# FP4 inner values turned by VectorE in 32x32 blocks and through HBM, their down-projection two chunks later, grid constants on ScalarE

## The chip, the cores and the metric

The kernel runs on one core of a Trainium2 chip. The metric is the device time of one execution in microseconds (us). Engines are named as in the profile: PE (TensorE) multiplies matrices, PEld is its weight load, DVE is VectorE, ACT is ScalarE, POOL is GpSimd, SP is the engine whose queue issues all DMAs here.

## The reference

Four batches of 1024 tokens with 256 features are layer-normed (xn). One branch is a linear attention with 8 heads and a gated network of 1024 inner values. The other is a gated network whose inputs, weights and inner values are rounded to FP4 in groups of 16. The output joins the two.

```python
def fp4_quant_dequant(x):                      # groups of 16 along the last dim
    scale = max(max(abs(group)) / 6.0, 1e-12)
    idx = searchsorted(_MID, abs(group / scale))
    return _GRID[idx] * sign(group) * scale    # grid 0, 0.5, 1, 1.5, 2, 3, 4, 6

xn = layernorm(x)
s  = x1 + silu(h @ Wgate) * (h @ Wup) @ Wdown  # x1 = xn + attention(rmsnorm(xn)), h = rmsnorm(x1), 1024 inner values
gate, y = fp4_linear(xn, w_gate), fp4_linear(xn, w_up)   # 704 inner values
g  = silu(fp4_linear(silu(gate) * y, w_down))  # the inner values are rounded to FP4 too
return x + s * g
```

## The kernel before

All matmuls work on values split in a high and a low part (HI, LO), three products for one: `split_product`, whose matmuls are line L248 in every view. The high part is rounded by ACT, the low part is what DVE subtracts.

The kernel has two stages. The first, some 610 us, goes through attention head by head; it also rounds the FP4 weights and the inputs and keeps what the second needs in HBM. The second, `networks`, goes through 8 blocks of 512 tokens (n), each of 4 chunks of 128 tokens (c). Of the plain network it makes two tiles of 128 inner values per chunk (f = 2c and 2c + 1, an even and an odd one, for all 512 tokens of the block); of the FP4 network it makes the 704 inner values of one chunk of tokens. Chunks of the FP4 network are numbered m = 4n + c, 0 to 31.

Each engine runs its own instruction list in the order written out by hand in `networks`; semaphores join them. One chunk on each engine:

- PE: `gate_up4` (FP4 gate and up, in two halves of 352 columns: two banks, B_GATE4 and B_UP4, each written by a half only when the half before was read, semaphores `s_gate4_ready` and `h4_ready`), `gate_up` of the even tile, `down` of the odd tile before, `turn4` (six 128x128 transposes of the quantized inner values of the chunk before, L759), `gate_up` of the odd tile, `down` of the even tile, `down4` (17 matmuls, FP4 down-projection of the chunk before).
- DVE: `product4` for both halves (L1440), `quantize_scale` (five steps, L1398 to L1402), `mlp_product` and `mlp_lo` of the even tile (L1429, L1433), `hq_lo` (L1446, low part of the turned chunk before, two parts), `quantize_constants` (L1406 takes the exponent bits, L1408 makes max(power, 1) * 1.5 * 2^22 of them, into `grid4`), `mlp_product` of the odd tile, `quantize_add` (L1411), `mlp_lo`, `quantize_subtract` (L1416), `quantize_done` (L1421 multiplies by the scale, L1422 repeats the last 64 columns). In chunk 0 the two halves of product4 for chunk 1 stand inside the chunk, ahead of `quantize_subtract` and at the end. Chunk 3 also has `xT_lo_of` (L1377, four operations on the next block's inputs) and the sum of the block with its residual (L1517).
- ACT: `silu4` (L1029), then for each tile silu of the gate and the rounding of the product (`mlp`, L1033 and L1035), `hq` (L1040, rounds the turned chunk), `gate_out` (L1046, silu of the FP4 network's output).
- POOL: products and sums of the output, four of each per block (L538, L542); at the start of the stage it makes the low part of `wdown` (L529).
- SP: loads the next inputs (`load_turned`, `load_xb`) and stores results.

At the end of the last block `last_down4` waits for the last chunk's transposes, and DVE makes the last products and sums. The steps that exchange blocks through HBM in the first stage (`exchange`: one store of 512 KB to `moved`, four loads of 128 KB) are of the kind that the change adds to the second.

Of the kernel before, what the change touches and what calls it, by code (L numbers as in the profile page):

```python
# [5 lines left out]
ALU = mybir.AluOpType  # L6
# [52 lines left out]
def build(nc, x, attn_w, Wq, Wk, Wv, Wo, out_w, mlp_w, Wgate, Wup, Wdown, w_gate, w_up, w_down, out):  # L59
# [32 lines left out]
                        for name in ("kept_xq", "kept_h2"))  # L92
    quant4 = nc.dram_tensor("quant4", (3 * NET4,), F32).ap()
# [5 lines left out]
    with ctx:  # L99
# [39 lines left out]
        eps = sb("eps", [P, 1], F32)  # L139
        warm = sb("warm", [P, 1], F32)  # L140
# [20 lines left out]
        x2 = one.cut(CH, ROW)  # L161
        state = one.cut(CH - 1, P)
# [35 lines left out]

        def as_tokens(row):
            return row.rearrange("p (c b t) -> p c b t", c=CH, b=QUADS)  # L200
# [28 lines left out]
        x2b = two.cut(CH, ROW)  # L229
        two.at = 0  # L230
# [96 lines left out]
        h4_turned, hq_hi, hqT_ready = sem("h4_turned"), sem("hq_hi"), sem("hqT_ready")  # L327
        out4_done, g4_ready = sem("out4_done"), sem("g4_ready")
# [4 lines left out]
        FIRST4 = min(T4, CH)  # L333
        FULL4, REST4 = N4 // P, N4 % P
# [17 lines left out]
        with nc.Block() as block:  # L352
            @block.sync
            def _(sp):
# [114 lines left out]
                def load_xb(n):  # L469
# [14 lines left out]
                sp.wait_ge(wdown_ready, 1)  # L484
                load_xb(0)
                sp.wait_ge(h2_turned, BLOCKS + 1)
                sp.dma_start(kept_h2[BLOCKS - 1].rearrange("a p x -> p a x"), leaving.rearrange("p a i x -> p a (i x)"))\
                  .then_inc(h2_stored, 16)

                for n in range(BLOCKS - 1):  # L490
                    if n + 2 < BLOCKS:
                        sp.wait_ge(xT_ready, (n + 1) * TURNS + KD)
                        load_turned(xq_in, kept_xq[n + 2], xq_loaded)
                        sp.wait_ge(xT_ready, (n + 1) * TURNS + TURNS)
                        sp.wait_ge(h2_stored, 16 * (n + 4))
                        load_turned(h2_in, kept_h2[n + 2], h2_loaded)
                    sp.wait_ge(res_ready, n + 1)
                    sp.dma_start(out_blocks[n], res).then_inc(out_stored, 16)
                    load_xb(n + 1)
# [7 lines left out]
            def _(pool):  # L507
                pool.memset(ident[:, :], 0.0).then_inc(s_const, 1)
                pool.memset(causal[:, :, :], 1.0).then_inc(s_const, 1)
                pool.memset(eps[:, :], EPS).then_inc(s_const, 1)  # L510
                pool.memset(leaving[:, :, 1, :], 0.0).then_inc(leaving_clear, 1)
                pool.wait_ge(s_const, 3)
# [15 lines left out]
                pool.wait_ge(wdown_hi, 1)  # L528
                pool.tensor_tensor(wdown[:, LO, :, :], raw_wdown, wdown[:, HI, :, :].bitcast(F32),  # L529
                                   ALU.subtract).then_inc(wdown_ready, 1)  # L530
# [15 lines left out]
            def _(pe):  # L546
# [44 lines left out]
                pe.wait_ge(s_const, 5)  # L591
# [131 lines left out]
                def down(n, f):  # L723
                    if f == 0:
                        pe.wait_ge(sum_read, n + 1)
                        pe.wait_ge(wdown_ready, 1)
                    pe.wait_ge(hmT_ready, n * FT + f + 1)
# [25 lines left out]
                def turn4(n, c):  # L753
                    pe.wait_ge(h4_quantized, n * CH + c + 1)
                    for f in range(T4):
                        if f == FIRST4:
                            pe.wait_ge(g4_ready, n * CH + c + 1)
                        bank = B_TURN4 if f < FIRST4 else B_OUT4
                        done = pe.transpose(ps[:, bank, (f % CH) * P:(f % CH + 1) * P],  # L759
                                            h4[:, c % 2, f * P:(f + 1) * P], ident[:, :])  # L760
# [3 lines left out]
                def down4(n, c):  # L764
                    pe.wait_ge(hqT_ready, (n * CH + c) * 2 + 2)
# [9 lines left out]
                def last_down4(n, c):  # L775
                    for f in range(T4):
                        if f in (0, FIRST4):
                            pe.wait_ge(hq_hi, (n * CH + c) * 2 + (1 if f == 0 else 2))
# [4 lines left out]
                    for f in range(T4):  # L783
                        if f in (0, FIRST4):
                            pe.wait_ge(hqT_ready, (n * CH + c) * 2 + (1 if f == 0 else 2))
# [36 lines left out]
                def networks(n, final):  # L822

                    for c in range(CH):
# [3 lines left out]
                        if c:  # L828
                            down(n, 2 * c - 1)
                            turn4(n, c - 1)  # L830
                        gate_up(n, 2 * c + 1)
                        down(n, 2 * c)
                        if c:
                            down4(n, c - 1)
                    down(n, FT - 1)
                    turn4(n, CH - 1)
                    if not final:
                        gate_up4(n + 1, 0)
                        down4(n, CH - 1)
                    else:  # L840
                        last_down4(n, CH - 1)
# [5 lines left out]
            def _(act):  # L847
# [104 lines left out]
                act.wait_ge(s_const, 5)  # L952
# [78 lines left out]
                def mlp(n, f):  # L1031
                    act.wait_ge(gate_done, n * FT + f + 1)
                    act.activation(s_gate, ps[:, B_GATE, :], ACT.Silu).then_inc(s_gate_ready, 1)  # L1033
                    act.wait_ge(hm_ready, n * FT + f + 1)
                    act.activation(hmT[:, f % 2, HI, :], hm, ACT.Copy).then_inc(hm_hi, 1)  # L1035

                def hq(n, c):
                    for i, (bank, f0, f1) in enumerate(((B_TURN4, 0, FIRST4), (B_OUT4, FIRST4, T4))):
                        act.wait_ge(h4_turned, (n * CH + c) * 2 + i + 1)
# [4 lines left out]
                def gate_out(n, c, bank=B_OUT4):  # L1044
                    act.wait_ge(out4_done, n * CH + c + 1)
                    act.activation(g4[:, c, :], ps[:, bank, 0:D], ACT.Silu).then_inc(g4_ready, 1)  # L1046
# [19 lines left out]
                act.activation(wdown[:, HI, :, :], raw_wdown, ACT.Copy).then_inc(wdown_hi, 1)  # L1066
                normed_h2(BLOCKS + 1, xq_new)

                def networks(n, final):
                    for c in range(CH):  # L1070
                        if c:
                            silu4(n, c)
                        mlp(n, 2 * c)
                        if c:
                            hq(n, c - 1)
                        if c == CH - 1 and not final:
                            xT_hi_of(n + 1, range(KD))
                        mlp(n, 2 * c + 1)
                        if c:
                            if c == 1:  # L1080
                                act.wait_ge(product_ready, n * CH + 1)
                            gate_out(n, c - 1)
# [478 lines left out]
```

## Time and profile before

| what | value |
|---|---|
| median of 3 runs | 1111.18 us (1109.03 to 1113.21) |
| profiled execution, its own time | 1108.42 us |
| its span | 1106.7 us |
| PE busy in the span | 1083.8 us (98%) |
| DVE busy | 906.8 us (82%) |
| ACT busy | 511.8 us (46%) |
| POOL busy | 52.2 us (5%) |
| granted clock of PE | 1.0 |

The views give times in us from the span's start. A row of the view in order of time has the start, the duration, the engine, the line, what is written from what, how many instructions were merged, and in brackets how long the engine stood idle before and who ended that. Matmuls are pipelined, so the distance between the starts of two groups tells what a group takes.

### The profile page before, as it was taken

To read this page: it belongs to the slowest core of one execution; us is meant where nothing else is said; L and a number is where in the kernel's file an instruction comes from. 1 tells how busy PE (TensorE), PEld (TensorE's weight loads), DVE (VectorE), ACT (ScalarE), POOL (GpSimd) and SP (SyncE) were. 2 spreads that over 40 slices of the span, in tenths; PEclk is the share of its full clock that TensorE was granted. 3 is DMA by queue.
4 is the path that set the end of the run, shared out by engine and by line. 5 is a ranking of instruction groups with operands and counts; after the bars stand their busy time and mean duration, and the time that the engine had idled before them with its cause. 6 is when DMAs were issued, how large, how long until landed. Compare 5 with 4: busy or idle time off the path is not lost.

```text
span 1106.7 us, 18820 instructions
## 1 busy us (share of the span) xinstructions
PE 1083.8 (98%) x7016; PEld 985.9 (89%) x7016; DVE 906.8 (82%) x1978; ACT 511.8 (46%) x1422; POOL 52.2 (5%) x71
## 2 busy tenths in 40 slices
PE   9999999999999999999998799999999999999997
PEld 6998999999989989999987699999999999999897
DVE  6888888898888988998677878878878778787786
ACT  6654646546546465465554533233323333233332
POOL 0000000000000000000000102020010202020200
PEclk9999999999999999999999999999999999999999
DMA  7455355454553554535447402011110203030010
GB/s 236 147 167 166 112 186 162 143 183 130 179 163 126 168 162 158 183 116 166 145 146 205 110 20 71 25 39 58 39 58 20 77 2 96 1 95 1 17 42 20
DMA packets 113466, 120.01 MB, mean 108 GB/s; under 512 B 8672, under 2 KB 108384, under 8 KB 113376
## 3 DMA queue, kind: packets, MB, share of 16 engines
q1 hardware_dynamic: 113376, 118.82, 34.0%
q8 instruction: 55, 0.90, 0.4%
q14 instruction: 35, 0.29, 0.1%
HBM read 65.75 MB, written 53.04 MB: 107 GB/s over the span
## 4 chain that ended last, share of the span: by engine, by line
PE 79%; DVE 12%; DMA 5%; ACT 2%; issue 1%; SPq 1%; POOL 0%; DVEq 0%; POOLq 0%
PE ps L248 59%; PE ps L638 4%; PE ps L679 4%; PE ps L673 4%; PE ps L659 3%; DMA moved<-work 3%; DMA r_gate<-moved 2%; PE ps L759 2%; PE ps L590 1%; DVE work L1429 1%; DVE r_k L1377 1%; DVE r_v L1433 1%; SPq L385 1%; DVE r_v L1446 1%; DVE work L1402 1%
## 5 line engine op out<-in xcount | busy, mean ns | idle before, releaser
L248 PE MATMUL ps<-r_k,r_gate_up 128*128 128x512 f32 x768 | 187.6, 394 | 4.0 <-DVE work L1429 3.3
L248 PEld LDWEIGHTS ps<-r_k,r_gate_up 128*128 128x128 f32 x768 | 141.0, 188 | 32.1 <-DVE work L1429 3.7
L248 PE MATMUL ps<-r_o,onT 128*128 128x256 f32 x768 | 107.0, 288 | 0.1
L898 ACT ACTIVATE work<-ps 128x128 f32<-128x128 f32 x256 | 67.4, 278 | 81.4 <-PE ps L679 81.4
L248 PEld LDWEIGHTS ps<-r_q,r_v 128*128 128x128 f32 x768 | 99.5, 191 | 5.9 <-issue 2.1
L248 PE MATMUL ps<-hT,r_k 128*128 128x512 f32 x378 | 103.2, 408 | 0.0
L248 PE MATMUL ps<-r_q,r_v 128*128 128x256 f32 x768 | 102.7, 283 | 0.0
L1035 ACT ACTIVATE r_v<-work 128x512 fp32r<-128x512 f32 x64 | 40.5, 633 | 131.9 <-DVE work L1429 131.9
L248 PE MATMUL ps<-hT,r_q 128*128 128x512 f32 x384 | 98.2, 391 | 0.0
L248 PE MATMUL ps<-r_v,hT 128*128 128x512 f32 x384 | 97.4, 390 | 0.0
L248 PEld LDWEIGHTS ps<-r_o,onT 128*128 128x128 f32 x768 | 95.7, 190 | 0.3 <-DVE onT L1157 0.3
L874 ACT ACTIVATE work<-ps 128x512 f32<-128x512 f32 x64 | 38.3, 599 | 121.8 <-PE ps L248 121.6
L248 PEld LDWEIGHTS ps<-hT,r_q 128*128 128x128 f32 x384 | 72.1, 188 | 16.4
L248 PEld LDWEIGHTS ps<-r_v,hT 128*128 128x128 f32 x384 | 72.1, 188 | 15.0
L1440 DVE TENSOR_TENSOR work<-ps,work 128x352 f32<-128x352 f32 x64 | 33.5, 523 | 56.9 <-PE ps L248 54.4
L248 PEld LDWEIGHTS ps<-hT,r_k 128*128 128x128 f32 x378 | 66.4, 189 | 11.1
L248 PE MATMUL ps<-r_gate,r_k 128*128 128x352 f32 x384 | 72.4, 324 | 2.7 <-ACT work L1029 2.7
L248 PE MATMUL ps<-r_up,r_k 128*128 128x352 f32 x384 | 72.3, 324 | 0.0
L679 PE MATMUL ps<-work 128*128 128x128 f32 x448 | 65.6, 284 | 3.9 <-DVE work L1347 2.9
L673 PE MATMUL ps<-work 128*128 128x128 f32 x512 | 67.7, 275 | 0.2 <-DVE work L1323 0.2
L638 PE MATMUL ps<-work 128*128 128x128 f32 x512 | 67.4, 274 | 0.0
L1033 ACT ACTIVATE work<-ps 128x512 f32<-128x512 f32 x64 | 38.3, 599 | 60.6 <-PE ps L248 60.6
(147 smaller groups left out, 2047.4 us busy)
## 6 DMA issues: line engine op xcount, KB each, us to landing
moved<-work SPq DMA_DIRECT2D x63, 512.0 KB, 2.9
r_gate<-moved SPq DMA_DIRECT2D x252, 128.0 KB, 2.6
work<-in_L_attn_hidden_states SPq DMA_DIRECT2D x16, 512.0 KB, 5.4
kept<-work SPq DMA_DIRECT2D x9, 514.0 KB, 4.4
kept_h<-work SPq DMA_DIRECT2D x9, 512.0 KB, 3.7
work<-kept SPq DMA_DIRECT2D x8, 514.0 KB, 6.1
kept_xq<-work SPq DMA_DIRECT2D x8, 512.0 KB, 5.8
work<-kept_xq SPq DMA_DIRECT2D x32, 128.0 KB, 2.8
```

The lines of the kernel that those rows point to most:

```text
L248: done = pe.matmul(out_ap, a, b, start=first and n == 0, stop=last and n == 2, skip_group_check=skip)
L385: sp.dma_start(arriving[q * QUAD:(q + 1) * QUAD].rearrange("p a i x -> p a (i x)"), moved[q].rearrange("(a p) x -> p a x", a=QUADS)).then_ ...
L638: done = pe.matmul(ps[:, B_SCORE, c * P:(c + 1) * P], kT[:, c * P:(c + 1) * P], qT[:, j % 2, c * P:(c + 1) * P], start=True, stop=True)
L659: done = pe.matmul(ps[:, B_STATE, c * P:(c + 1) * P], k_tok[:, c, :], v_sb[:, half, c, hv:hv + P], start=True, stop=True)
L673: pe.matmul(ps[:, B_O, c * P:(c + 1) * P], attn[:, c, :], v_sb[:, half, c, hv:hv + P], start=c == 0, stop=s == 0 and c == 0, skip_group_ch ...
L679: done = pe.matmul(ps[:, B_O, c * P:(c + 1) * P], qT[:, j % 2, c * P:(c + 1) * P], before, start=False, stop=True, skip_group_check=True)
L759: done = pe.transpose(ps[:, bank, (f % CH) * P:(f % CH + 1) * P], h4[:, c % 2, f * P:(f + 1) * P], ident[:, :])
L874: act.activation(kT, ps[:, B_K, :], ACT.Copy).then_inc(k_ready, 1)
L898: done = act.activation(squares[:, c, :], ps[:, B_O, c * P:(c + 1) * P], ACT.Square, accum_out=small[:, OS, c:c + 1])
L1033: act.activation(s_gate, ps[:, B_GATE, :], ACT.Silu).then_inc(s_gate_ready, 1)
L1035: act.activation(hmT[:, f % 2, HI, :], hm, ACT.Copy).then_inc(hm_hi, 1)
L1440: dve.tensor_tensor(h4[:, c % 2, e * HALF4:(e + 1) * HALF4], ps[:, B_UP4, 0:HALF4], s_gate4[:, e, :], ALU.mult).then_inc(h4_ready, 1)
```

## The change

- `turn4` goes. In `quantize_done` DVE turns the rescaled chunk itself, in blocks of 32x32 with two transposes (640 columns, and the last 64 columns read twice for 128); SP stores the result to a buffer in HBM (`kept_h4`, two of them in turn) and loads it back in four parts with the blocks in their turned places (`exchange4`). The last chunk, m = 31, is still turned by PE (`last_turn4`).
- `down4` of a chunk runs two chunks later (LAG4 = 2), so `hq`, `hq_lo` and `gate_out` do too. `hq` and `hq_lo` are one operation of 768 columns each, from SBUF. `gate_out` of a block's first chunk waits for the output products of the block before.
- `grid4` is made by ACT (`grid4_on_act`: Relu(power * GRID - GRID), the bias from a column of memory), behind the even tile's work and ahead of the odd tile's silu. DVE adds GRID back in the add and the subtract, which become two-step operations; the sign is turned by the subtract, and the scale is made negative for it.
- The low part of `wdown` is made by DVE in two halves instead of POOL, and ACT rounds it in two halves.
- SP's order is written anew around `exchange4`.

```diff
+                def exchange4(m):
+                    through = kept_h4[m % 2]
+                    sp.wait_ge(h4_quantized, m + 1)
+                    sp.dma_start(through.rearrange("a p x -> p a x"), h4_turned_sb).then_inc(hq_stored, 16)
+                    sp.wait_ge(hq_stored, 16 * (m + 1))
+                    if m:
+                        sp.wait_ge(hqT_ready, m)
+                    for q in range(QUADS):
+                        sp.dma_start(hq_in[q * QUAD:(q + 1) * QUAD],
+                                     through[q].rearrange("(b p) x -> p b x", b=QUADS)).then_inc(hq_loaded, 16)
+                for n in range(BLOCKS):
+                    exchange4(n * CH)
...
+                    exchange4(n * CH + 1)
+                    if n:
+                        sp.wait_ge(res_ready, n)
+                        sp.dma_start(out_blocks[n - 1], res).then_inc(out_stored, 16)
+                        load_xb(n)
+                    exchange4(n * CH + 2)
...
-                pool.tensor_tensor(wdown[:, LO, :, :], raw_wdown, wdown[:, HI, :, :].bitcast(F32),
-                                   ALU.subtract).then_inc(wdown_ready, 1)
...
-                            turn4(n, c - 1)
                         gate_up(n, 2 * c + 1)
                         down(n, 2 * c)
-                        if c:
-                            down4(n, c - 1)
+                        if n * CH + c >= LAG4:
+                            down4(n * CH + c - LAG4)
                     down(n, FT - 1)
-                    turn4(n, CH - 1)
                     if not final:
                         gate_up4(n + 1, 0)
-                        down4(n, CH - 1)
                     else:
-                        last_down4(n, CH - 1)
+                        for m in range(LAST4 + 1 - LAG4, LAST4):
+                            down4(m)
+                        last_turn4()
+                        last_down4()
...
+                def hq(m):
+                    act.wait_ge(hq_loaded, 16 * QUADS * (m + 1))
+                    if m:
+                        act.wait_ge(out4_done, m)
+                    act.activation(hqT[:, HI, :, :].rearrange("p f (a t) -> p f a t", t=QUAD), turned4_sb(hq_in), ACT.Copy)\
+                       .then_inc(hq_hi, 1)
+                def grid4_on_act(m):
+                    act.wait_ge(power4_ready, m + 1)
+                    act.activation(grid4, grid4, ACT.Relu, scale=GRID, bias=minus_grid[:, 0:1]).then_inc(grid4_ready, 1)
...
-                    settled2(dve.tensor_scalar(grid4.bitcast(U32), data.bitcast(U32), EXPONENT, None,
-                                               ALU.bitwise_and), mine)
-                    settled2(dve.tensor_scalar(grid4, grid4, 1.0, 1.5 * 2.0 ** 22, ALU.max, ALU.mult), mine)
+                    dve.tensor_scalar(grid4.bitcast(U32), data.bitcast(U32), EXPONENT, None,
+                                      ALU.bitwise_and).then_inc(power4_ready, 1)
...
-                    dve.tensor_tensor(data, data, grid4, ALU.add).then_inc(dve2, 1)
+                    dve.wait_ge(grid4_ready, m + 1)
+                    dve.scalar_tensor_tensor(data, grid4, GRID, data, ALU.add, ALU.add).then_inc(dve2, 1)
...
+                    dve.transpose(to[:, 0:FULL4], data[:, 0:split].rearrange("p (f a t) -> p f a t", a=QUADS, t=QUAD))
+                    rest = data[:, split:N4].rearrange("p (d a t) -> p d a t", d=1, t=QUAD)
+                    dve.transpose(to[:, FULL4].rearrange("p (d a) t -> p d a t", d=2),
+                                  rest.to_broadcast([P, 2, QUADS // 2, QUAD])).then_inc(h4_quantized, 1)
...
+                def wdown_lo(i):
+                    dve.wait_ge(wdown_hi, i + 1)
```

DVE's list for a chunk 1, from the even tile's mlp_product to the end of the chunk. Before:

```order
L1429 TENSOR_TENSOR work<-ps,work 128x512
L1433 TENSOR_TENSOR r_v<-work,r_v 128x512
L1446 TENSOR_TENSOR r_v<-ps,r_v 128x512
L1446 TENSOR_TENSOR r_v<-ps,r_v 128x256
L1406 TENSOR_SCALAR work<-work 128x704
L1408 TENSOR_SCALAR work<-work 128x704
L1429 TENSOR_TENSOR work<-ps,work 128x512
L1411 TENSOR_TENSOR work<-work 128x704
L1433 TENSOR_TENSOR r_v<-work,r_v 128x512
L1416 TENSOR_TENSOR work<-work 128x704
L1421 TENSOR_TENSOR work<-work 128x704
L1422 COPY work<-work 128x64
```

DVE's list at the same place, now (L1500 is mlp_product, L1504 mlp_lo, L1516 hq_lo, L1467 the mask):

```order
L1500 TENSOR_TENSOR work<-ps,work 128x512
L1504 TENSOR_TENSOR r_v<-work,r_v 128x512
L1516 TENSOR_TENSOR r_v<-work,r_v 128x768
L1467 TENSOR_SCALAR work<-work 128x704
L1500 TENSOR_TENSOR work<-ps,work 128x512
L1472 SCALAR_TENSOR_TENSOR work<-work 128x704
L1504 TENSOR_TENSOR r_v<-work,r_v 128x512
L1477 SCALAR_TENSOR_TENSOR work<-work 128x704
L1482 TENSOR_TENSOR work<-work 128x704
L1490 STREAM_TRANSPOSE work<-work 128x5x4x32
L1492 STREAM_TRANSPOSE work<-work 128x4x32
```

The multiply L1408 left the list, the two parts of hq_lo became one, and two transposes stand at the end in the place of the copy.

ACT's list for a chunk without extras, from silu4 to gate_out. Before:

```order
L1029 ACTIVATE work<-ps 128x352 x2
L1033 ACTIVATE work<-ps 128x512
L1035 ACTIVATE r_v<-work 128x512
L1040 ACTIVATE r_v<-ps 128x512
L1040 ACTIVATE r_v<-ps 128x256
L1033 ACTIVATE work<-ps 128x512
L1035 ACTIVATE r_v<-work 128x512
L1046 ACTIVATE work<-ps 128x256
```

ACT's list at the same place, now (L1069 is the silu of a tile, L1079 hq, L1084 the grid):

```order
L1065 ACTIVATE work<-ps 128x352 x2
L1069 ACTIVATE work<-ps 128x512
L1079 ACTIVATE r_v<-work 128x768
L1073 ACTIVATE r_v<-work 128x512
L1084 ACTIVATE work<-work,minus_grid 128x704
L1069 ACTIVATE work<-ps 128x512
L1073 ACTIVATE r_v<-work 128x512
L1098 ACTIVATE work<-ps 128x256
```

The grid stands between the even tile's rounding and the odd tile's silu, and hq moved ahead of the even tile's rounding.

PE's list at the end of the program, from the last chunk's second gate_up. Before:

```order
L248 MATMUL ps<-r_k,r_gate_up 128x512 x12
L248 MATMUL ps<-r_q,r_v 128x256 x12
L248 MATMUL ps<-r_o,r_v 128x256 x15
L771 MATMUL ps<-r_o,r_v 128x256 x2
L248 MATMUL ps<-r_q,r_v 128x256 x12
L759 MATMUL ps<-ident,work 128x128 x6
L781 MATMUL ps<-r_o,r_v 128x256 x11
L786 MATMUL ps<-r_o,r_v 128x256 x6
```

PE's list at the same place, now:

```order
L258 MATMUL ps<-r_k,r_gate_up 128x512 x12
L258 MATMUL ps<-r_q,r_v 128x256 x12
L258 MATMUL ps<-r_o,r_v 128x256 x15
L807 MATMUL ps<-r_o,r_v 128x256 x2
L258 MATMUL ps<-r_q,r_v 128x256 x12
L258 MATMUL ps<-r_o,r_v 128x256 x15
L807 MATMUL ps<-r_o,r_v 128x256 x2
L794 MATMUL ps<-ident,work 128x128 x6
L817 MATMUL ps<-r_o,r_v 128x256 x11
L822 MATMUL ps<-r_o,r_v 128x256 x6
```

A down4, that of chunk 30, came between the last mlp product and the last chunk's transposes.

## Rows read from the trace of the kernel before

**Rows 1.** Busy time of each engine in a stretch of the second stage, all engines:

```profile
core 0: us, PE busy (x) PEld busy (x) DVE busy (x) ACT busy (x) POOL busy (x), PEclk, DMA share, GB/s
645.00:1090.00 445.00, 443.62 (x2808) 409.99 (x2807) 346.96 (x598) 149.14 (x294) 43.92 (x56) 1.00 0.13 40
```

**Rows 2.** In order of time, PE, one chunk: start, us, operation, idle:

```profile
828.89 2.91 PE L248 MATMUL ps<-r_k,r_gate_up 128*128 128x512 f32 x12
831.64 1.60 PE L248 MATMUL ps<-r_q,r_v 128*128 128x256 f32 x12
833.07 0.81 PE L759 MATMUL ps<-ident,work 128*128 128x128 f32 x6
833.64 3.01 PE L248 MATMUL ps<-r_k,r_gate_up 128*128 128x512 f32 x12
836.49 1.60 PE L248 MATMUL ps<-r_q,r_v 128*128 128x256 f32 x12
```

**Rows 3.** In order of time, DVE, the same chunk:

```profile
827.19 0.53 DVE L1440 TENSOR_TENSOR work<-ps,work 128x352 f32<-128x352 f32 x1 [1.10 <-PE ps L248]
829.09 0.53 DVE L1440 TENSOR_TENSOR work<-ps,work 128x352 f32<-128x352 f32 x1 [1.38 <-PE ps L248]
829.65 0.89 DVE L1398 TENSOR_REDUCE work<-work 128x44 f32<-128x704 f32 x1
...
832.40 0.69 DVE L1429 TENSOR_TENSOR work<-ps,work 128x512 f32<-128x512 f32 x1
833.79 0.69 DVE L1433 TENSOR_TENSOR r_v<-work,r_v 128x512 fp32r<-128x512 f32 x1 [0.70 <-ACT r_v L1035]
834.40 1.01 DVE L1446 TENSOR_TENSOR r_v<-ps,r_v 128x512 fp32r<-128x512 f32 x2
835.33 0.52 DVE L1406 TENSOR_SCALAR work<-work 128x704 uint32<-128x704 uint32 x1
...
836.75 0.69 DVE L1429 TENSOR_TENSOR work<-ps,work 128x512 f32<-128x512 f32 x1 [0.34 <-PE ps L248]
...
839.68 0.89 DVE L1421 TENSOR_TENSOR work<-work 128x704 f32<-128x704 f32 x1
...
842.09 0.53 DVE L1440 TENSOR_TENSOR work<-ps,work 128x352 f32<-128x352 f32 x1 [1.28 <-PE ps L248]
```

**Rows 4.** In order of time, DVE, sums of two blocks, inputs of the next:

```profile
676.88 1.22 DVE L1517 TENSOR_TENSOR work<-ps,work 128x1024 f32<-128x1024 f32 x1
...
850.23 1.29 DVE L1377 TENSOR_TENSOR r_k<-work,r_k 128x512 fp32r<-128x512 f32 x2
...
857.72 1.22 DVE L1517 TENSOR_TENSOR work<-ps,work 128x1024 f32<-128x1024 f32 x1
```

**Rows 5.** Groups by line and shape, whole span: count, busy us, mean ns, idle:

```profile
L1224 DVE STREAM_TRANSPOSE work<-work 128x512 f32<-128x512 f32 x34 | 21.5, 672 | 0.0
L1188 DVE SCALAR_TENSOR_TENSOR r_gate_up<-work,nw_mlp,r_gate_up 128x512 fp32r<-128x512 f32 x8 | 5.9, 741 | 0.0
L922 ACT ACTIVATE work<-work 128x256 f32<-128x256 f32 x36 | 15.2, 496 | 0.0
L943 ACT ACTIVATE r_o<-work,nw_out 128x2048 fp32r<-128x2048 f32 x1 | 2.0, 2007 | 0.0
```

**Rows 6.** In order of time, POOL and DVE, where they meet:

```profile
744.89 2.80 POOL L542 TENSOR_TENSOR work<-work 128x256 f32<-128x256 f32 x4
...
747.28 0.97 DVE L1433 TENSOR_TENSOR r_v<-work,r_v 128x512 fp32r<-128x512 f32 x1 [0.70 <-ACT r_v L1035]
```

**Rows 7.** DMA issues by line: count, KB each, median us from issue to landing:

```profile
moved<-work SPq DMA_DIRECT2D x63, 512.0 KB, 2.9
r_gate<-moved SPq DMA_DIRECT2D x252, 128.0 KB, 2.6
```

**Rows 8.** In order of time, POOL and DVE, the start of the second stage:

```profile
619.37 4.56 POOL L529 TENSOR_TENSOR r_q<-work,r_q 128x2048 fp32r<-128x2048 f32 x1 [26.04 <-ACT r_q L1066]
...
620.13 3.85 DVE L1399 TENSOR_SCALAR work<-work 128x44 f32<-128x44 f32 x1
```

More of the change, by code:

```diff
@@ L161, in build @@
         x2 = one.cut(CH, ROW)
+        x2_end = one.at
         state = one.cut(CH - 1, P)
@@ L197, in landed, with turned4_sb @@
             return tile.rearrange("p (b k c t) -> p k c b t", b=QUADS, k=KD, c=CH)[:, k]
+        def turned4_sb(tile):
+            return tile.rearrange("p a (f t) -> p f a t", t=QUAD)
         def as_tokens(row):
@@ L229, in build @@
         x2b = two.cut(CH, ROW)
+        two.at = max(two.at, x2_end)
+        h4_turned_sb = two.cut(QUADS, T4 * QUAD)
+        hq_in = work[:, down4_at:down4_at + QUADS * T4 * QUAD].rearrange("p (a x) -> p a x", a=QUADS)
         two.at = 0
@@ L333, in build @@
         FIRST4 = min(T4, CH)
+        LAG4 = 2
+        LAST4 = BLOCKS * CH - 1
         FULL4, REST4 = N4 // P, N4 % P
@@ L726, in down @@
                         pe.wait_ge(wdown_ready, 1)
+                    if n == 0 and f == FT // 2:
+                        pe.wait_ge(wdown_ready, 2)
                     pe.wait_ge(hmT_ready, n * FT + f + 1)
@@ L1042, in hq, with gate_out @@
                            .then_inc(hq_hi, 1)
-                def gate_out(n, c, bank=B_OUT4):
-                    act.wait_ge(out4_done, n * CH + c + 1)
-                    act.activation(g4[:, c, :], ps[:, bank, 0:D], ACT.Silu).then_inc(g4_ready, 1)
+                def gate_out(m, bank=B_OUT4):
+                    if m % CH == 0 and m:
+                        act.wait_ge(product_ready, m + 1)
+                    act.wait_ge(out4_done, m + 1)
+                    act.activation(g4[:, m % CH, :], ps[:, bank, 0:D], ACT.Silu).then_inc(g4_ready, 1)
                 def weights4_hi(i, k):
@@ L1065, in _ @@
                 act.wait_ge(wdown_loaded, 16)
-                act.activation(wdown[:, HI, :, :], raw_wdown, ACT.Copy).then_inc(wdown_hi, 1)
+                for f in range(0, FT, FT // 2):
+                    act.activation(wdown[:, HI, f:f + FT // 2, :], raw_wdown[:, f:f + FT // 2, :], ACT.Copy)\
+                       .then_inc(wdown_hi, 1)
                 normed_h2(BLOCKS + 1, xq_new)
@@ L1070, in networks @@
                     for c in range(CH):
+                        earlier = n * CH + c - LAG4
                         if c:
                             silu4(n, c)
-                        mlp(n, 2 * c)
-                        if c:
-                            hq(n, c - 1)
+                        silu_gate(n, 2 * c)
+                        if LAG4 == 2 and earlier >= 0:
+                            hq(earlier)
+                        hmT_hi(n, 2 * c)
                         if c == CH - 1 and not final:
                             xT_hi_of(n + 1, range(KD))
[L1078 to L1082, printed above, removed]
+                        grid4_on_act(n * CH + c)
+                        silu_gate(n, 2 * c + 1)
+                        if LAG4 == 1 and earlier >= 0:
+                            hq(earlier)
+                        hmT_hi(n, 2 * c + 1)
+                        if earlier >= 0:
+                            gate_out(earlier)
                     if not final:
                         xT_hi_of(n + 1, range(KD, TURNS))
-                    hq(n, CH - 1)
-                    if not final:
                         silu4(n + 1, 0)
-                    gate_out(n, CH - 1, B_GATE if final else B_OUT4)
+                    else:
+                        for m in range(LAST4 + 1 - LAG4, LAST4):
+                            hq(m)
+                            gate_out(m)
+                        last_hq()
+                        gate_out(LAST4, B_GATE)
                 for n in range(BLOCKS - 1):
@@ L1477, in _ @@
                 product4(0, 0, 1)
+                def wdown_lo(i):
+                    dve.wait_ge(wdown_hi, i + 1)
+                    part = slice(i * FT // 2, (i + 1) * FT // 2)
+                    dve.tensor_tensor(wdown[:, LO, part, :], raw_wdown[:, part, :], wdown[:, HI, part, :].bitcast(F32),
+                                      ALU.subtract).then_inc(wdown_ready, 1)
+                wdown_lo(0)
                 DVE_BLOCK = CH * (SCALE_STEPS + ROUND_STEPS)
@@ L1512, in networks @@
                     if final:
-                        hq_lo(n, CH - 1)
+                        for m in range(LAST4 + 1 - LAG4, LAST4):
+                            hq_lo(m)
+                        last_hq_lo()
                     dve.wait_ge(mlp_done, n + 1)
@@ L1519, in networks @@
                     if not final:
-                        hq_lo(n, CH - 1)
                         product4(n + 1, 0, 0)
```

104 lines of the change are left out of this document (63 added, 41 removed).

## The prediction, made before the changed kernel was run

> **What bounds the kernel now.** I read the busy times of the second stage first (the networks, some 445 of 1106.7 us): PE is busy for 443.6 of 445 us, DVE for 347, ACT for 149 [rows 1]. So PE sets the pace there, and a matmul taken off PE is time won, as long as nobody else becomes the pace. DVE's 78% looks like room. Whether it is room is not told by a share but by the order, so next I read one chunk in order of time on PE and on DVE.
>
> PE: twelve 512-column products take 2.75 us (828.89 to 831.64), twelve 256-column products 1.43, the six transposes 0.57 (833.07 to 833.64), and the twelve 512-column products behind them 2.85, 0.10 more than the others [rows 2]. A transposed chunk thus costs PE 0.67 us. DVE: from one chunk's first product4 to the next is 14.90 us (827.19 to 842.09), and in it DVE waits 1.28 and 1.38 us for PE at product4's halves, 0.34 at the second mlp_product, and 0.70 for ACT at mlp_lo [rows 3]. A block of four chunks takes (857.72 - 676.88) / 3 = 60.28 us [rows 4]. So DVE's real room is about 3 us in a chunk, and only where it waits for PE.
>
> **The change, part by part.** All times are for the steady blocks; there are seven periods from block to block.
>
> *PE loses turn4*: 0.67 us per chunk. PE alone would need 14.90 - 0.67 = 14.23 per chunk, 56.9 per block.
>
> *DVE, one chunk walked again in the new order*, from product4's first half to the next chunk's first half. The first half (0.53) frees the bank, PE makes the second up product (half of the 1.90 between 827.19 and 829.09, 0.95), and DVE starts 0.20 after its end (829.09 against 828.89): 1.68 when DVE comes last, where 1.90 was PE's pace. Second half 0.56, scales 2.75, mlp_product and ACT's rounding 1.39, mlp_lo 0.61, all as before [rows 2, 3]. hq_lo is one operation of 768 columns: from 512 columns at 0.69 and 704 at 0.89 [rows 3] a column is 1.04 ns, so 0.96, less 0.08 that operations in a row overlap (0.69 long, 0.61 apart): 0.88, where the two parts took 0.93. The mask takes 0.52 as before.
>
> Then comes **the new wait**. ACT makes the grid constants only when the mask is there, and silu_gate of the odd tile is queued behind it on ACT, so mlp_product of that tile waits on DVE for both. The grid is 704 columns with a pointer: 256 such columns take 0.496, 2048 take 2.007, so 0.84 ns a column and 0.87 us [rows 5]. silu_gate is another ACT operation of 512 columns, 0.70 with both hops, as the wait at 833.79 shows [rows 3]; operations in a row overlap a little, so I take 1.50 together. Before, mlp_product waited 0.34 for PE there and ACT had its silu ready. The multiply taken from DVE (from the mask's end at 835.85 to 836.41, where that wait begins: 0.56) gives back a third of this. Queued behind the wait on DVE are the whole rounding, the transposes and the next chunk's product4, for which PE's up product waits.
>
> Product, add, mlp_lo, subtract: 2.93 (836.75 to 839.68), with the add and the subtract in their two-step form taken as equal; the nearest row is 0.741 against 0.69 at 512 columns, so up to 0.06 more for each [rows 3, 5]. Rescaling 0.92. The transposes: 512 columns take 0.672 [rows 5], so 640 take 0.81 and 128 take 0.27, less the overlap 0.91 together; before, the copy of 64 columns hid in the wait for PE. Sum: 1.68 + 0.56 + 2.75 + 1.39 + 0.61 + 0.88 + 0.52 + 1.50 + 2.93 + 0.92 + 0.91 = **14.65**. That is over PE's 14.23: DVE's round now sets the pace, and PE waits for h4_ready.
>
> *The block.* Chunks 0 and 1 have one product4 round trip between them, since chunk 1's halves are made inside chunk 0: 2 x 14.65 - (1.68 + 0.56) + 0.44 + 0.55 = 28.05. Within chunk 0 PE's own way to that product is 0.53 + 0.95 + 5.50 + 1.43 + 2.03 (17 matmuls at 0.12) + 1.90 + 0.20 = 12.54 after product4, and DVE is there at 11.90, so 0.64 more: 28.69. Chunk 2: 14.65. Chunk 3 has four xT_lo of 0.60 and the sum of 1.13 besides [rows 4]: 18.2. Together 61.5.
>
> *POOL.* Its products and sums of the output now come one chunk later, and the last product meets DVE in back-to-back operations on two SBUF operands. Today four sums run from 744.89 to 747.69, and mlp_lo that starts at 747.28 takes 0.97 instead of 0.69: it stood still until POOL was done [rows 3, 6]. That is 0.28 today, in time DVE had to spare. I take one POOL instruction of 0.7 (2.80 / 4) in DVE's way per block, so 0.6; bounds 0 and 2.
>
> By the Trainium skill (SBUF — State Buffer, "SBUF: two separate sides") whoever starts first holds the shared ports for a whole instruction, and it names two-operand VectorE operations against GpSimd's; the row above agrees. By it the worst case is all five instructions, 5 x 0.7 = 3.5 per block; whether a transpose is held up too no row here shows.
>
> So a block takes 61.5 + 0.6 = 62.1, against 60.28: +1.85, and +13 over seven.
>
> *The exchange* through HBM is hidden. A store takes 2.9 us and loads 2.6 [rows 7]; the loads wait for hq_lo of the chunk before, and ACT needs them one chunk later less hq_lo's own way there (rounding, mlp_lo, hq_lo, some 4 us), so about 10 us cover 2.6 and the issue of four. If that cover went, each us beyond it would cost 1 us in each of 31 chunks. SP's other transfers (res, x, the turned inputs) stand between the exchanges, with a chunk or more to their use.
>
> *Start*: today POOL's 4.56 us for wdown's low part holds a DVE scalar operation of 44 columns for 3.85 [rows 8]. The change gives that back, but puts two halves of 1024 columns (1.2 each, at 1.04 ns a column) on DVE, and chunks 0 and 1 of block 0 have the new wait and the transposes too. I take 0, within 2 either way. *Tail*: down4 of chunk 30 now stands between the last mlp product and the last chunk's transposes, with its hq_lo ahead of it: 2.03 + 0.88 = 2.9.
>
> Sum: 13 + 0 + 2.9 = **+16 us**. The profiled execution (1108.42, span 1106.7) would be 1124; it ran 2.8 under the median of 1111.18, so the median comes to **1127**.
>
> By the Trainium skill (VectorE: DVE Perf Modes, "Rules for kernel authors") a 128x128 transpose belongs on TensorE when PSUM may take it, which speaks against the change. Op for op the trace agrees: 0.67 on PE against 0.91 on DVE; it doesn't decide, since PE is the full engine today.
>
> **Rivals.**
> *DVE's room is enough, PE stays the bound.* For it: 3 us of waits per chunk on DVE today. The block is then 56.9, 3.4 less, times seven plus the tail: 1111 - 24 + 3 = 1090. It needs a DVE round of at most 14.23 in every chunk and room for the block's extras (3.5 us), so some 1.2 us less per chunk than I count; it would hold if silu of the odd tile didn't stand behind the grid on ACT. It does in ACT's order. Chance 0.07.
> *A tie.* Transposes at 0.72 (the small one hidden), the grid at 0.79, no POOL in the way: 0.27 less per chunk and 0.6 per block, a block of 60.4, and the tail remains: 1115. Chance 0.14.
> *Worse.* The transposes write pieces of 32 columns far apart; should they take 1.3, two-step add and subtract 0.06 more each and POOL 2 per block, the block is 62.1 + 4 x 0.5 + 1.4 = 65.5: 1111 + 37 + 3 = 1151; half of that 1139. Chance 0.11.
>
> **How the numbers follow.** My forecast, DVE's round with the wait for ACT as the bound, has 0.68 and 1127, with its own ends at about 1117 and 1137. The range 1113 to 1139 leaves out the first rival, the low half of the tie and the far half of the worse case, about 0.2. Within 0.5% (5.6 us, about what a measurement of this kernel can tell from none) lie most of the tie and little else: same 0.13; faster is the first rival, 0.07; slower 0.80.
>
> **What would show it.** In the trace of the changed kernel: mlp_product of the odd tile waits about 1.5 us for ACT's silu in each chunk, where it waited 0.34 for PE; product4's first half of chunks 2 and 3 no longer waits for PE, and PE waits there for product4; the block's sum on DVE comes every 62 us; PE is busy for less than 97% of the stage. hq on ACT waits for no transfer. I'm wrong if product4 still waits over 0.5 us for PE in its first half (then PE is the bound and the time falls), if ACT waits for the loads, or if the transposes take much other than 0.8 and 0.27.

## The result, and the profile after

The changed kernel takes 1137.49 us (median, 1136.23 to 1140.1) where the kernel before takes 1110.11 in the same comparison: 1.0261 times as long, interval 1.024 to 1.0281. It is slower, as forecast, by 27 us where 16 were forecast. Its profiled execution took 1136.23 us, with a span of 1134.5 us.

The busy times of the second stage, the view of [rows 1], here for the changed kernel (the columns are the same; the last two stretches are 2 and 3.5 us of one chunk):

```profile
core 0: us, PE busy (x) PEld busy (x) DVE busy (x) ACT busy (x) POOL busy (x), PEclk, DMA share, GB/s
650.00:1100.00 450.00, 417.41 (x2494) 376.03 (x2492) 340.02 (x540) 160.06 (x280) 52.00 (x56) 0.98 0.28 85
...
834.90:836.90 2.00, 1.98 (x7) 1.98 (x8) 0.00 (x0) 0.00 (x0) 0.44 (x1) 0.50 0.55 197
836.80:840.30 3.50, 3.50 (x14) 2.84 (x14) 3.04 (x6) 1.26 (x2) 0.00 (x0) 0.81 0.02 5
```

PE is busy for 92.8% of the stage, where it was 99.7%: it is no longer what sets the pace. DVE is at 76% and doesn't look full either. As in [rows 1], the share hides what the order shows. DVE in order of time, from the even tile's mlp_product of chunk 1 to the scales of the next chunk, answers [rows 3]:

```profile
823.72 0.69 DVE L1500 TENSOR_TENSOR work<-ps,work 128x512 f32<-128x512 f32 x1
825.11 0.69 DVE L1504 TENSOR_TENSOR r_v<-work,r_v 128x512 fp32r<-128x512 f32 x1 [0.70 <-ACT r_v L1073]
825.72 0.95 DVE L1516 TENSOR_TENSOR r_v<-work,r_v 128x768 fp32r<-128x768 f32 x1
826.59 0.52 DVE L1467 TENSOR_SCALAR work<-work 128x704 uint32<-128x704 uint32 x1
828.61 0.69 DVE L1500 TENSOR_TENSOR work<-ps,work 128x512 f32<-128x512 f32 x1 [1.50 <-ACT work L1069]
829.22 0.88 DVE L1472 SCALAR_TENSOR_TENSOR work<-work 128x704 f32<-128x704 f32 x1
830.02 0.68 DVE L1504 TENSOR_TENSOR r_v<-work,r_v 128x512 fp32r<-128x512 f32 x1
830.62 1.43 DVE L1477 SCALAR_TENSOR_TENSOR work<-work 128x704 f32<-128x704 f32 x1
832.08 1.30 DVE L1482 TENSOR_TENSOR work<-work 128x704 f32<-128x704 f32 x1
833.42 0.84 DVE L1490 STREAM_TRANSPOSE work<-work 128x640 f32<-128x640 f32 x1
834.19 0.27 DVE L1492 STREAM_TRANSPOSE work<-work 128x128 f32<-128x128 f32 x1
834.38 0.48 DVE L1511 TENSOR_TENSOR work<-ps,work 128x352 f32<-128x352 f32 x1
837.09 0.53 DVE L1511 TENSOR_TENSOR work<-ps,work 128x352 f32<-128x352 f32 x1 [2.22 <-PE ps L258]
```

Three things are to be seen. The odd tile's mlp_product waits 1.50 us for silu (ACT L1069), where it waited 0.34 for PE. The first half of product4 (834.38) waits for nobody, where it waited 1.10 and 1.28 for PE. And the subtract and the rescaling take 1.43 and 1.30 us here, where the same two-step form takes 0.88 in the add two rows above and the rescaling took 0.89 before. Beside them POOL is at work, seen in order of time:

```profile
830.32 0.98 POOL L571 TENSOR_TENSOR work<-work 128x256 f32<-128x256 f32 x1 [13.43 <-ACT work L1098]
831.26 4.07 POOL L575 TENSOR_TENSOR work<-work 128x256 f32<-128x256 f32 x4
```

The subtract starts beside the last product, the rescaling runs beside the sums. The same four sums took 2.80 in [rows 6]. PE in order of time, the place that waits for product4's first half, with the same place of the block before ahead of it (the rows of [rows 2] no longer have their twin, since the transposes are gone):

```profile
771.59 1.23 PE L258 MATMUL ps<-r_up,r_k 128*128 128x352 f32 x6 [2.45 <-DVE work L1511]
772.65 2.91 PE L258 MATMUL ps<-r_k,r_gate_up 128*128 128x512 f32 x12
775.40 1.60 PE L258 MATMUL ps<-r_q,r_v 128*128 128x256 f32 x12
...
831.36 1.11 PE L258 MATMUL ps<-r_gate,r_k 128*128 128x352 f32 x6
834.92 2.13 PE L258 MATMUL ps<-r_up,r_k 128*128 128x352 f32 x6 [2.45 <-DVE work L1511]
836.85 3.51 PE L258 MATMUL ps<-r_k,r_gate_up 128*128 128x512 f32 x12
840.20 1.60 PE L258 MATMUL ps<-r_q,r_v 128*128 128x256 f32 x12
```

Both times PE stands idle for 2.45 us. At 771.59 it goes on as it was: the six matmuls take 1.06 (to 772.65), the twelve behind them 2.75. At 834.92 the six take 1.93 and the twelve 3.35, at a granted clock of 0.50 in the first 2 us (the second stretch of the table above): the lower of the two levels, 1.2 GHz instead of 2.4. DVE's second half, which needs the six, then waits 2.22, where it waited 1.32 after 771.59.

Where the slow stretch lies differs from block to block. In the block ahead of these two, PE goes on at 707.14 after the same wait; the six matmuls still take 1.06, and the twelve behind them 4.34. DVE then waits for the twelve, at the even tile's mlp_product:

```profile
712.80 0.69 DVE L1500 TENSOR_TENSOR work<-ps,work 128x512 f32<-128x512 f32 x1 [1.13 <-PE ps L258]
```

The block sum (L1606) starts at 675.26, 739.70, 803.05, 867.36, 931.87, 996.32, 1060.78 and 1127.43. So a block takes (1060.78 - 675.26) / 6 = 64.25 us, against 60.28 [rows 4]; 63.35 in the one block without the clock's fall, 64.3 to 64.5 in the five others. The last block, which is not among the six, has a fall too (granted clock 0.50 from 1095 to 1097).

### The profile page after: what moved, and what is told of

It reads as the page before. It is cut to its first block, busy times and chain, and to the rows that moved or that the text cites. A ratio compares the mean times of both kernels' runs of the same rounds, so it can differ in the third digit from the quotient of the medians.

```text
span 1134.5 us, 18698 instructions
## 1 busy us (share of the span) xinstructions
PE 1079.8 (95%) x6830; PEld 974.0 (86%) x6830; DVE 914.4 (81%) x1948; ACT 533.6 (47%) x1424; POOL 55.7 (5%) x71
## 4 chain that ended last, share of the span: by engine, by line
PE 65%; DVE 25%; ACT 5%; issue 3%; DMA 2%; SPq 0%; DVEq 0%
PE ps L258 47%; PE ps L671 5%; PE ps L706 4%; PE ps L712 4%; PE ps L692 4%; DVE work L1482 2%; DVE work L1500 2%; DVE work L1477 2%; DVE r_v L1504 2%; DVE work L1511 2%; DVE r_k L1438 2%; DVE work L1463 1%; DVE work L1459 1%; ACT work L1084 1%; DVE r_v L1516 1%
## 5 line engine op out<-in xcount | busy, mean ns | idle before, releaser
L258 PE MATMUL ps<-r_k,r_gate_up 128*128 128x512 f32 x768 | 198.3, 409 | 2.1 <-DVE work L1500 2.0
L258 PEld LDWEIGHTS ps<-r_k,r_gate_up 128*128 128x128 f32 x768 | 148.6, 199 | 36.4 <-DVE work L1500 7.6
L258 PE MATMUL ps<-r_up,r_k 128*128 128x352 f32 x384 | 76.7, 337 | 26.6 <-DVE work L1511 26.6
L258 PEld LDWEIGHTS ps<-r_up,r_k 128*128 128x128 f32 x384 | 63.8, 193 | 31.9 <-DVE work L1511 31.2
L1500 DVE TENSOR_TENSOR work<-ps,work 128x512 f32<-128x512 f32 x64 | 44.2, 691 | 54.6 <-ACT work L1069 48.2
L1069 ACT ACTIVATE work<-ps 128x512 f32<-128x512 f32 x64 | 37.7, 589 | 98.8 <-PE ps L258 98.8
L706 PE MATMUL ps<-work 128*128 128x128 f32 x512 | 67.7, 275 | 0.2 <-DVE work L1384 0.2
L712 PE MATMUL ps<-work 128*128 128x128 f32 x448 | 65.1, 283 | 2.8 <-DVE work L1408 2.7
```

Of the source, the lines that this page charges most:

```text
L258: done = pe.matmul(out_ap, a, b, start=first and n == 0, stop=last and n == 2, skip_group_check=skip)
L706: pe.matmul(ps[:, B_O, c * P:(c + 1) * P], attn[:, c, :], v_sb[:, half, c, hv:hv + P], start=c == 0, stop=s == 0 and c == 0, skip_group_ch ...
L712: done = pe.matmul(ps[:, B_O, c * P:(c + 1) * P], qT[:, j % 2, c * P:(c + 1) * P], before, start=False, stop=True, skip_group_check=True)
L1500: dve.tensor_tensor(hm, ps[:, B_UP, :], s_gate, ALU.mult).then_inc(hm_ready, 1)
```

## The experiments

Two theories are held against each other. **A**: DVE's round is the pace, made too long above all by the wait for silu behind the grid; POOL and PE's clock add to it. **B**: the new operations themselves are what costs (the turning on DVE, the exchange, the two-step forms), wherever silu stands. Kernels that undo or mend one part are told as edits of the changed kernel, those that make one part alone as edits of the kernel before. The kernel before took 1107.83 us beside four of them (silu ahead of the grid, grid back on DVE, no POOL, filler on PE) and 1109.35 beside the other four.

**silu ahead of the grid on ACT.** (The added wait is one that is always met by then.)

```diff
-                        grid4_on_act(n * CH + c)
                         silu_gate(n, 2 * c + 1)
+                        grid4_on_act(n * CH + c)
...
+                    if f % 2:
+                        dve.wait_ge(hmT_ready, n * FT + f)
```

> The changed kernel with one line moved on ScalarE: the odd tile's silu ahead of the grid constants. Theory A (VectorE's round is the pace, and the grid in front of the odd tile's silu is its largest new part): the 1.5 us wait of mlp_product in each chunk falls to about 0.3 at the add, a chunk's round from 14.65 to about 13.4, under TensorE's 14.23; a block comes down from 64.4 to 58.5 to 60, the time to 1093 to 1108, no slower than the kernel before. Rival B (the turning itself is the loss, by VectorE's transposes, the transfers and what they hold up): a block stays over 62.5, the time over 1122.

It took 1104.01 us, ratio 0.9965 (0.9942 to 0.9989); a block takes 59.93 (671.41 to 791.26, two blocks). DVE, the same place as above, odd tile's mlp_product to product4:

```profile
815.29 0.68 DVE L1502 TENSOR_TENSOR work<-ps,work 128x512 f32<-128x512 f32 x1
816.33 0.89 DVE L1472 SCALAR_TENSOR_TENSOR work<-work 128x704 f32<-128x704 f32 x1 [0.36 <-ACT work L1084]
817.14 0.68 DVE L1506 TENSOR_TENSOR r_v<-work,r_v 128x512 fp32r<-128x512 f32 x1
817.74 0.88 DVE L1477 SCALAR_TENSOR_TENSOR work<-work 128x704 f32<-128x704 f32 x1
818.66 1.31 DVE L1482 TENSOR_TENSOR work<-work 128x704 f32<-128x704 f32 x1
```

mlp_product waits no more, and the grid now comes 0.36 late for the add. That is 1.14 less in each of four chunks, PE's wait in chunk 2 is 0.77 instead of 2.45, no fall of the clock follows it, and a block is 4.3 us shorter than the changed kernel's 64.25. B is out as the main cause: turning, exchange and two-step forms are all still there. DVE is still late in places: the 0.77 us are a wait for product4 (up product at 821.51).

**The grid back on DVE**, the rest of the change as it is:

```diff
-                        grid4_on_act(n * CH + c)
...
+                    settled2(dve.tensor_scalar(grid4, grid4, 1.0, GRID, ALU.max, ALU.mult), mine)
...
-                    dve.scalar_tensor_tensor(data, grid4, GRID, data, ALU.add, ALU.add).then_inc(dve2, 1)
+                    dve.scalar_tensor_tensor(data, grid4, 0.0, data, ALU.add, ALU.add).then_inc(dve2, 1)
```

> The changed kernel with the grid constants made by VectorE again (two operations, as before), all else as changed: blocks turned through HBM, down-projection two chunks later. A: the wait of 1.5 goes, 0.56 of work comes back, a chunk's round 13.7; a block about 60, the time 1102 to 1110, about the kernel before. B: the turning alone is slower than before by 15 us or more.

1108.15 us, ratio 0.9993 (0.9968 to 1.0018), block 60.41 (672.41 to 793.24, two). So turning on DVE with the exchange neither costs nor wins, within 0.3% and with the wdown part in it, which is worth some 2 us by itself (below). The groups of PE by shape, from 676 us on, say why nothing is won:

```profile
L258 PE MATMUL ps<-r_up,r_k 128*128 128x352 f32 x324 | 61.8, 326 | 12.9 <-DVE work L1510 12.9
```

PE has no transposes left, but it waits 12.9 us for product4, some 2.0 in a block (0.97 in chunk 0 and 1.00 in chunk 2): most of the 4 x 0.67 that it was given goes into waiting.

**The grid on ACT alone**, in the kernel before: `grid4_on_act(n * CH + c)` ahead of `mlp(n, 2 * c + 1)`, and the add and the subtract in their two-step forms.

> The kernel before with the grid constants on ScalarE alone (as in the change, ahead of the odd tile's silu; two-step add and subtract), transposes on TensorE, down-projection one chunk later as before. A: the wait adds some 0.9 to VectorE's chunk, which the 1.1 to 1.3 of its wait for TensorE at product4 takes in; only at the block's end, where TensorE waits for the quantized chunk 3, it shows: 0 to 0.9 per block, the time 1107 to 1115. If the wait costs its length wherever it stands: 31 x 0.9 = 28 more, 1136.

1116.02 us, ratio 1.0073 (1.0045 to 1.0101), block 61.43 (675.39 to 798.26, two), 1.15 more than before: a little past the 0.9 and the 1115 us that I expected at most. The wait is the same one, as DVE in order of time shows; the first row is the first half of a product4, the second the odd tile's mlp_product after it:

```profile
828.74 0.53 DVE L1449 TENSOR_TENSOR work<-ps,work 128x352 f32<-128x352 f32 x1 [0.38 <-PE ps L249]
...
838.90 0.69 DVE L1438 TENSOR_TENSOR work<-ps,work 128x512 f32<-128x512 f32 x1 [1.50 <-ACT work L1037]
```

Here product4 still waits for PE (0.38 where it was 1.10): the wait for silu was paid for the most part out of DVE's room. Taken apart, then, the turning (with the rest of the change) costs nothing and the grid on ACT 0.7%; together they cost 2.6%. Each alone about fits into the same room of DVE, and both don't.

**wdown's low part on DVE alone**, in the kernel before:

```diff
-                pool.tensor_tensor(wdown[:, LO, :, :], raw_wdown, wdown[:, HI, :, :].bitcast(F32),
-                                   ALU.subtract).then_inc(wdown_ready, 1)
...
+                wdown_lo(0)
```

> The kernel before with only the low part of wdown made by VectorE in two halves instead of GpSimd. The prediction took the start at 0, within 2. A: the 3.85 us stand of the 44-column operation goes, 2.3 of work come: the time 1 to 3 less, 1105 to 1107. If two halves on VectorE cost more than the stand: 1108 to 1111.

1106.98 us, ratio 0.9979 (0.9964 to 0.9994). The first block, from the second half of its first product4 to its sum, takes 56.55 (617.43 to 673.98) where it took 58.23 before (618.65 to 676.88): this part of the change is worth some 2 us by itself.

**No POOL in blocks 0 to 6.** The kernel leaves out POOL's products and sums there, so the output of these blocks is not made; all waits and transfers stay.

```diff
-                        pool.tensor_tensor(res[:, c, :], res[:, c, :], g4[:, c, :], ALU.mult).then_inc(product_ready, 1)
+                        pool.sem_inc(product_ready, 1)
...
-                        done = pool.tensor_tensor(res[:, c, :], res[:, c, :], xb[:, c, :], ALU.add)
-                    done.then_inc(res_ready, 1)
+                    pool.sem_inc(res_ready, 1)
```

> The changed kernel without GpSimd's output products and sums in the blocks 0 to 6 (that part of the output is left out; all waits and transfers stay). A: the subtract and the rescaling of chunk 1 take 0.9 each instead of 1.43 and 1.30, TensorE's wait ahead of chunk 2's second up product falls from 2.45 to about 1.5, its clock stays at 2.4 GHz there, and a block takes 62.2 to 62.6 instead of 64.4: the time about 1123. If the clock falls all the same: about 63.4 and 1130. If GpSimd has no part in it: 1137.

1124.41 us, ratio 1.013 (1.0066 to 1.0194), block 62.41 (676.69 to 801.51, two). DVE's two operations are back at 0.89, PE waits 1.50 instead of 2.45, and no fall of the clock follows (DVE, then PE, in order of time):

```profile
829.12 0.89 DVE L1476 SCALAR_TENSOR_TENSOR work<-work 128x704 f32<-128x704 f32 x1
830.04 0.89 DVE L1481 TENSOR_TENSOR work<-work 128x704 f32<-128x704 f32 x1
...
832.47 1.23 PE L258 MATMUL ps<-r_up,r_k 128*128 128x352 f32 x6 [1.50 <-DVE work L1510]
833.53 2.91 PE L258 MATMUL ps<-r_k,r_gate_up 128*128 128x512 f32 x12
```

**Filler on PE while it waits**, ten matmuls of 512 columns into a bank that nobody reads:

```diff
+                            if c == 2 and e == 1 and w is wup4:
+                                for _ in range(10):
+                                    pe.matmul(ps[:, B_TURN4, :], wgate[:, HI, 0, 0:P], h2T[:, HI, 0, :],
+                                              start=True, stop=True)
```

> The changed kernel with ten matmuls of 512 columns more in each block, into a bank nobody reads, between the two products of chunk 2 for whose second one TensorE waits 2.45 us: the wait is filled, nothing else moves. If the fall of the clock behind this wait costs what the blocks with and without it differ by (64.4 against 63.35): a block 63.3, granted clock 1.0, the time about 1129. If the slow matmuls behind the wait have another cause: 64.4 and 1137 or more.

1131.71 us, ratio 1.019 (1.0145 to 1.0234), block 63.37 (676.41 to 803.14, two): the block as expected, the time some 3 us over the 1129 expected. PE in order of time:

```profile
832.40 2.46 PE L779 MATMUL ps<-r_k,r_gate_up 128*128 128x512 f32 x10
835.02 1.23 PE L258 MATMUL ps<-r_up,r_k 128*128 128x352 f32 x6 [0.15 <-DVE work L1515]
836.09 2.89 PE L258 MATMUL ps<-r_k,r_gate_up 128*128 128x512 f32 x12
```

The up product comes no earlier, but takes 1.07, and the block is as long as the changed kernel's one block without a fall (63.35). With the two kernels the block comes apart: 62.41 for DVE's round without POOL, 63.37 - 62.41 = 0.96 for POOL in DVE's way, and 64.43 - 63.37 = 1.06 for the clock in the five blocks in which it fell.

**No transposes at all**, in the kernel before. The kernel leaves them out, so its FP4 branch goes on with what stands in the banks:

```diff
-                        done = pe.transpose(ps[:, bank, (f % CH) * P:(f % CH + 1) * P],
-                                            h4[:, c % 2, f * P:(f + 1) * P], ident[:, :])
                         if f == FIRST4 - 1 or f == T4 - 1:
-                            done.then_inc(h4_turned, 1)
+                            pe.sem_inc(h4_turned, 1)
```

> The kernel before without the transposes of turn4 on TensorE (left out: its output for the FP4 branch is made from what stands in the banks; all waits, copies and the order stay). A: TensorE's 0.67 per chunk was real and VectorE of the kernel before has room for it: a block 57 to 57.8 instead of 60.28, the time 1083 to 1090. That is what the turning could have won. If VectorE's room isn't enough even there, a block stays over 59 and the time over 1098.

1097.24 us, ratio 0.9896 (0.9861 to 0.993), block 58.94 (676.22 to 794.09, two). This missed what I expected: 4 x 0.67 = 2.7 leave PE in a block, and only 1.3 are won. PE's groups show waits for DVE that the kernel before didn't have:

```profile
L248 PE MATMUL ps<-r_q,r_v 128*128 128x256 f32 x672 | 90.4, 284 | 2.1 <-DVE r_v L1430 2.1
L248 PE MATMUL ps<-r_up,r_k 128*128 128x352 f32 x336 | 63.5, 324 | 1.2 <-DVE work L1437 0.9
L248 PE MATMUL ps<-r_gate,r_k 128*128 128x352 f32 x334 | 62.8, 323 | 4.0 <-DVE work L1419 4.0
```

Together 7.3 us, 1.0 in a block: with PE's work gone and nothing put on DVE, DVE is already late at the block's end. So with DVE's list as it was before, the transposes could be worth no more than some 12 us, however they were replaced.

**Both orders mended**: silu first, and the first half of the next product4 ahead of the transposes in chunks 1 and 2 and ahead of the block sum in chunk 3, so that PE gets its bank earlier.

```diff
+                    if between is not None:
+                        between()
...
-                            product4(n, c, 0)
...
-                        quantize_done(c, n * CH + c, mine)
+                        quantize_done(c, n * CH + c, mine, (lambda: product4(n, c + 1, 0)) if c in (1, 2) else None)
...
+                    if not final:
+                        product4(n + 1, 0, 0)
                     dve.wait_ge(mlp_done, n + 1)
...
-                        product4(n + 1, 0, 0)
```

> The changed kernel with the odd tile's silu ahead of the grid (as in the first experiment) and the first half of the next chunk's product4 ahead of the transposes in chunks 1 and 2 and ahead of the block's sum at its end, so that what VectorE does behind it fills the round trip to TensorE. A (TensorE waits for that half because it stands behind 0.9 or 1.1 us of work nobody on TensorE needs): TensorE's waits for product4 go, a block 57.2 to 58.5 instead of 59.9, the time 1086 to 1094, faster than both kernels. If something else holds TensorE there: 59.9 and 1104.

1091.26 us, ratio 0.9843 (0.9818 to 0.9869): 1.6% below the kernel before, and below the changed one. A block takes 57.94 (672.49 to 788.36, two). The busy times of its second stage:

```profile
645.00:1070.00 425.00, 424.60 (x2611) 386.64 (x2610) 352.95 (x566) 168.84 (x293) 45.28 (x56) 1.00 0.31 96
```

PE is busy for 99.9% again, and 60.28 - 4 x 0.67 = 57.6 is what was left for it. So the 0.67 per chunk was there to be had; DVE's order had kept it from PE.

## Why the prediction was wrong: the mechanism held, the size failed

*What held.* The kernel became slower, and the pace went from PE to DVE, by the wait for the grid and silu: 1.50 forecast, 1.50 measured. The grid took 0.884 against 0.87, hq_lo 0.95 against 0.96, the two-step forms 0.88 as taken (equal to the one-step form), the transposes 0.845 and 0.269 against 0.81 and 0.27. Without POOL in DVE's way a block takes 62.41, which lies 0.9 over the 61.5 that the prediction walked to. About that much is the sum of small terms: a product4 round trip of 1.80 instead of 1.68 (831.93 to 833.73 without POOL), three times; the transposes 0.96 net instead of 0.91, four times; and 0.91 instead of 0.64 for PE in chunk 0. The exchange is hidden: the store takes 2.6 us, a load 2.3, and ACT's hq waits for no load.

*What failed* is the size, 27 instead of 16: a block was forecast at 62.1 and took 64.25, and the start was forecast at nothing. From the kernel before to the changed one, the block sum of the last block came 27.8 us later in the profiled executions (1127.43 against 1099.61). They fall so:

- Six periods: 6 x (64.25 - 60.28) = 23.8, forecast 6 x 1.85 = 11. The step that was mis-sized is "one POOL instruction of 0.7 in DVE's way per block, so 0.6": it was 0.96, since two DVE operations were hit and not one. The step that is missing altogether is the clock. I counted PE's waiting as nothing more than DVE's lateness; after 2.45 us of it PE made some of its next products at half speed, in five blocks of six, and DVE waits for just these: 1.06 in each of the five. 61.5, the 0.9 of small terms, 0.96 and 1.06 make the 64.4 of the five blocks. Over the six periods the clock is 5.3 us, the small terms 5.4, and what POOL took beyond its 0.6 is 2.2.
- The start: "I take 0, within 2". The first block took 61.02 from the second half of its first product4 to its sum (614.24 to 675.26), against 58.23: +2.8, more than the 2 allowed. The wdown part alone makes it 1.7 shorter, so the rest of the change costs 4.5 there, if the two simply add; 0.94 of it is DVE's wait for PE behind another fall of the clock (mlp_product at 648.36). The first stage ended 4.4 earlier in this execution (614.24 against 618.65), which hides the miss in this pair of traces. That is luck: the end lies between 614.0 and 618.8 in the kernels shown here, at 614.01 too in the kernel before with the grid alone, and what moves it stays open.
- The last block and the tail: +5.6, of which 4.0 are a block like the others. That leaves 1.6 where 2.9 were forecast; what of the 2.9 was hidden there was not tried.

By the ratio the result (1.0261 times 1111.18 is 1140) lies just past the range's upper end of 1139. The range's upper side came from the "worse" rival, which had transposes of 1.3 in it, POOL 2 and no clock. Its parts were wrong, and the forecast's own end of 1137 had no term for what PE does after a wait.

*The rival "PE stays the bound, 1090"* named its own condition, that silu should not stand behind the grid. With that alone the time is 1104, because product4 still stands behind the transposes and the block sum on DVE. With product4 moved too it is 1091, at a block of 57.94 where the rival had 56.9; so that the two times agree to 1 us is in part luck.

*The 3 us of room* on DVE in a chunk were too generous: they were the waits for PE, counted without asking what is late next at the block's end. The kernel without transposes shows half of PE's gain already lost there.

## What to carry to other kernels

Where an engine's work is given to another, ask what stands behind it in the other's list: 0.88 us of grid on a lightly loaded ACT stood ahead of a silu that DVE needed, and exchanging the two gave back 33 us. Room on the engine that receives work is spent once: parts that each cost 0 or 0.7% alone cost 2.6% together. Before work is taken off the full engine, take first what it would wait for next (here the product that frees its bank) out from behind work that nobody waits for. And where the full engine is made to wait, read what it does after the wait: here a wait of 2.45 us brought 1.06 us more, in five blocks of six.

## What the hardware showed that I hadn't expected

*PE's clock.* In a stage where PE is otherwise busy, PE waits 2.45 us at the same place in each of the six periods. In five of them the granted clock fell to 0.50, at the latest some 1.3 us after PE went on; in the sixth (771.59) it stayed at 1.0. After waits of 1.50 (the kernel without POOL) no fall was seen at this place, and filler matmuls in the wait held the clock. The length of the wait alone doesn't decide: in the first block of the filler kernel a wait of 1.96 us (PE goes on at 635.40) came with a fall, six 128x512 matmuls taking 2.73 us, and in the kernel before a wait of 3.30 us (PE goes on at 626.37) came with none, the same six taking 1.50. What decides between fall and none is left open. The Trainium skill (TensorE: Matmul & The Clock Gate, "Part 1: The HAM clock gate") tells of these two levels and that PE's idle time brings the lower one. The rows above agree on the levels, with 1.93 us for six matmuls that take 1.06 at full clock. Each of the falls named here came at a wait of PE, but not every wait brought one.

*DVE and POOL.* With POOL's last product and its four sums beside them (the sums 4.07 us instead of 2.80) two DVE operations in a row took 1.43 and 1.30 instead of 0.88 and 0.89, so both engines were slowed. The transposes that ran while POOL was still at its sums (833.42 to 834.46, POOL until 835.33) took their 0.84 and 0.27. That answers what the prediction left open. By the Trainium skill (SBUF — State Buffer, "SBUF: two separate sides") it is DVE operations with two SBUF inputs that share a port with POOL; the trace agrees, since the transposes have one.
